# Second attention of a four-layer model: where batches 2 and 3 are summed and normalised, and in which order

## The reference

```python
x = x + _L0_ffn_ref(_layernorm(x, axis=-1), ...)            # the sum that ends layer 0
x = x + _L1_xattn_ref(ctx_1024, ctx_1024, _layernorm(x, axis=-1), mask, L1_xattn_Wv, ..., L1_xattn_bo)

def _layernorm(x, axis=-1, eps=1e-05):
    m = jnp.mean(x, axis=axis, keepdims=True)
    v = jnp.var(x, axis=axis, keepdims=True)
    return (x - m) / jnp.sqrt(v + eps)

def _L1_xattn_ref(values, keys, queries, mask, Wv, Wk, Wq, Wo, bo):   # 16 heads of 8 columns
    ...
    energy = jnp.where(mask == 0, jnp.float32(-1e+20), energy)
    attn = jax.nn.softmax(energy * (1.0 / E ** 0.5), axis=3)
    out = jnp.einsum('nhqk,nkhd->nqhd', attn, v).reshape(N, Sq, E)
    return out @ Wo.T + bo
```

## Time and profile before

| | us |
|---|---|
| median of three timed runs | 1225.13 |
| lowest and highest | 1221.35, 1225.40 |
| the profiled execution | 1229.93 |
| its span, first to last instruction | 1228.1 |
| TensorE busy in the span | 1054.8 (86%) |
| VectorE busy | 722.0 (59%) |
| ScalarE busy | 644.5 (52%) |
| GpSimd busy | 565.4 (46%) |
| mean granted clock of TensorE | 0.929 of full |

### The profile page before, as it was taken

How to read it: one execution, slowest core, us unless ns; L and a number is a source line. 1 busy time by engine, 2 the same in 40 slices (tenths; PEclk the granted TensorE clock), 3 DMA queues, 4 the chain that set the end, 5 groups by cost and what they waited for, 6 DMA issues and landing times.

```text
span 1228.1 us, 22204 instructions
## 1 busy us (share of the span) xinstructions
PE 1054.8 (86%) x6815; PEld 797.5 (65%) x6815; DVE 722.0 (59%) x2456; ACT 644.5 (52%) x2117; POOL 565.4 (46%) x918
## 2 busy tenths in 40 slices
PE   4988999669889978879999997776799999977994
PEld 3775789635556657756767665665667776654994
DVE  5574454487676772286767784322776676852444
ACT  2343333347778714358778762222387888731231
POOL 5223665350000152557555656365375555655452
PEclk9988999979999999899999997698799999986997
DMA  2003556589500124110000001363300000004666
GB/s 63 13 26 120 161 179 205 164 148 408 188 1 1 36 63 141 50 33 19 1 19 18 1 4 44 85 185 121 86 19 1 2 1 1 2 31 124 193 209 180
DMA packets 116004, 102.86 MB, mean 84 GB/s; under 512 B 18027, under 2 KB 97571, under 8 KB 115888
## 3 DMA queue, kind: packets, MB, share of 16 engines
q1 hardware_dynamic: 105280, 82.71, 23.1%
q0 software_dynamic: 8448, 17.20, 4.2%
q10 hardware_dynamic: 2160, 1.53, 0.5%
HBM read 65.04 MB, written 36.36 MB: 83 GB/s over the span
## 4 chain that ended last, share of the span: by engine, by line
PE 57%; DVE 17%; issue 6%; ACT 6%; another core or an unknown queue 4%; DMA 4%; POOL 3%; SPq 2%; DVEq 0%; ACTq 0%; POOLq 0%
PE ps L2952 4%; PE ps L2756 4%; PE ps L2758 4%; PE ps L2848 4%; PE ps L2757 4%; PE ps L2966 4%; PE ps L2861 4%; PE ps L3493 3%; PE ps L3497 3%; PE ps L3147 2%; PE ps L3506 2%; PE ps L2980 2%; ACT ex L1301 2%; DVE ln_st L1705 2%
## 5 line engine op out<-in xcount | busy, mean ns | idle before, releaser
L1301 ACT ACTIVATE ex<-ps,nmx 128x154 f32<-128x154 f32 x512 | 194.5, 393 | 73.9 <-DVE nmx L2257 72.3
L1085 POOL TENSOR_TENSOR pp<-ex,rc 128x256 f32<-128x256 f32 x256 | 157.7, 616 | 145.7 <-DVE rc L2262 144.8
L2257 DVE TENSOR_REDUCE nmx<-ps 128x2 f32<-128x308 f32 x256 | 119.5, 470 | 59.4 <-PE ps L2758 58.8
L922 POOL DMA_INDIRECT yq_d<-yq,ids_q x78 | 74.7, 958 | 79.5 <-DVE yq L2007 61.5
L2952 PEld LDWEIGHTS ps<-ident,pp 128*128 128x128 f32 x640 | 73.7, 141 | 56.5 <-POOL pp L1086 47.6
L2756 PE MATMUL ps<-kp,q_s 128*128 128x308 f32 x256 | 95.6, 374 | 12.9 <-ACT ex L1301 11.8
L1301 ACT ACTIVATION_READ_ACCUMULATOR ex<-ps,nmx 128x1 f32 x512 | 105.4, 206 | 0.0
L1418 ACT ACTIVATE pe<-ps,nmx 128x154 f32<-128x154 f32 x256 | 85.1, 394 | 37.1 <-DVE nmx L2138 36.0
L2952 PE MATMUL ps<-ident,pp 128*128 128x128 f32 x640 | 99.9, 280 | 3.8 <-POOL pp L1086 3.7
L892 POOL TENSOR_TENSOR ln_r<-ln_v,mhalf 128x4 f32<-128x4 f32 x32 | 33.2, 1036 | 112.3 <-DVE ln_v L1713 91.7
L2848 PE MATMUL ps<-xc_q,w_q 128*128 128x256 f32 (+1 forms) x276 | 63.5, 370 | 19.9 <-issue 13.8
(11 more groups left out here) (477 smaller groups left out, 2836.9 us busy)
## 6 DMA issues: line engine op xcount, KB each, us to landing
w_r<-in_L_ffn_W SPq DMA_DIRECT2D x69, 256.0 KB
xq_d<-blankq SPq DMA_DIRECT2D x4, 4160.0 KB, 23.8
w_q<-in_L_ffn_W SPq DMA_DIRECT2D x46, 256.0 KB
w_q<-in_L_ffn_w SPq DMA_DIRECT2D x46, 128.0 KB
xq<-xq_d SPq DMA_DIRECT2D x24, 130.0 KB
w_s<-in_L_ffn_W SPq DMA_DIRECT2D x8, 256.0 KB
w_e<-in_L_ffn_W SPq DMA_DIRECT2D x8, 256.0 KB, 4.7
acc<-yq_d SPq DMA_DIRECT2D x8, 256.0 KB, 4.4
```

The costliest lines, as they stand in the source:

```text
L922: pool.indirect_dma_start(yq_d[:, :], bass.IndirectOffsetOnAxis(ap=ids_q[:, c:c + 1], axis=0), yq[k % NY][:, h, :], None).then_inc(q_out[k ...
L1085: pool.tensor_tensor(pp[st % 2][:, m % 4, 2 * j:2 * j + 2, :], w[:, :, 0:P], r.broadcast_to([P, 2, P]), ALU.mult)
L1301: ins = act.activation(ex[:, tt % NEX, j, :], ps[:, tt % 3, j * SK:(j + 1) * SK], ACT.Exp, bias=nmx8[:, tt % 8, j:j + 1], accum_out=sm8[:, ...
L2257: dve.tensor_reduce(nmx8[:, tt % 8, :], ps[:, tt % 3, 0:2 * SK].rearrange("p (h s) -> p h s", h=2), AX.X, ALU.max, negate=True).then_inc(n ...
```

## The change

GpSimd adds batch 2's and batch 3's shares to `x_tok` (`whole_sum`) and writes their normalised rows (`normed`: power, product with `row_any`, subtraction of the mean, multiplication). VectorE keeps the statistics of these batches and waits for `x_new` in place of summing. VectorE packs batch 0's queries before it scales batch 1. The maxima and statistics are put in another order: batch 2's statistics behind the maxima of m = 2, batch 3's behind those of m = 6. Batch 1's transposes move behind the scores of m = 2, batch 2's to the end of step 0, and batch 3's into step 1, in front of `queries(2)`. The output bias is added in steps 1 to 4 (`out_bias`), and the blank rows are set in step 1.

```diff
--- before.py
+++ after.py
@@ -503,7 +503,7 @@
         ln_shift = z_bm
         c_hi_ok = sem("c_hi_ok"); c_ok = sem("c_ok")
         n_raw = [sem("n_raw0"), sem("n_raw1")]; n_wk0 = sem("n_wk0"); n_wo1 = sem("n_wo1"); n_wo = sem("n_wo"); n_zero = sem("n_zero"); n_kz = sem("n_kz")
-        n_x = sem("n_x"); n_xl = sem("n_xl")
+        n_n = sem("n_n"); n_xl = sem("n_xl")
         n_full = sem("n_full"); n_hi = sem("n_hi"); n_fa = sem("n_fa"); n_fd = sem("n_fd")
         n_s = sem("n_s"); n_m = sem("n_m"); n_e = sem("n_e"); n_r = sem("n_r"); n_z = sem("n_z")
         n_va = sem("n_va"); n_pv = sem("n_pv"); n_oh = sem("n_oh"); n_ol = sem("n_ol"); n_on = sem("n_on"); n_pr = sem("n_pr")
@@ -1086,20 +1086,42 @@
                     pool.tensor_tensor(pp[st % 2][:, m % 4, 4, :].rearrange("p (h c) -> p h c", h=4)[:, 2 * j:2 * j + 2, 0:SK - P],
                                        w[:, :, P:SK], r.broadcast_to([P, 2, SK - P]), ALU.mult).then_inc(n_z, 1)
 
+                def whole_sum(b):
+
+                    pool.wait_ge(p_add, B + 2 * (b - 1))
+                    pool.tensor_tensor(x_tok[:, tiles(b), :], x_tok[:, tiles(b), :], acc[:, bsl(b)].rearrange("p (n d) -> p n d", n=TB), ALU.add).then_inc(x_new, 1)
+
+                def normed(b):
+
+                    rstd(2, b)
+                    pool.wait_ge(ln_rstd, B * 2 + b + 1)
+                    pool.tensor_tensor(ln_r[:, tiles(b)], ln_r[:, tiles(b)], row_any[:, tiles(b)], ALU.mult).then_inc(n_n, 1)
+                    pool.tensor_tensor(xn_tok[:, tiles(b), :], x_tok[:, tiles(b), :], ln_mv[:, tiles(b), 0:1].broadcast_to([P, TB, D]), ALU.subtract).then_inc(n_n, 1)
+                    pool.wait_ge(n_n, 2 * (b - 1))
+                    pool.tensor_tensor(xn_tok[:, tiles(b), :], xn_tok[:, tiles(b), :], ln_r[:, tiles(b)].rearrange("p (n a) -> p n a", a=1).broadcast_to([P, TB, D]), ALU.mult).then_inc(ln_ok, 1)
+
+                def out_bias(b):
+
+                    pool.wait_ge(ln_ok, B * 2 + b + 1)
+                    pool.tensor_tensor(x_tok[:, tiles(b), :], x_tok[:, tiles(b), :], bo1[:, :].rearrange("p (a d) -> p a d", a=1).broadcast_to([P, TB, D]), ALU.add).then_inc(p_add, 1)
+
                 if l == 1:
                     rstd(2, 0)
                     pool.wait_ge(ln_ok, B * 2 + 1)
                     add_second(2)
                     rstd(2, 1)
+                    pool.wait_ge(ln_ok, B * 2 + 2)
+                    whole_sum(2)
                     add_second(3)
-                    rstd(2, 2)
-                    rstd(2, 3)
-                    for b in range(B):
-                        pool.wait_ge(ln_ok, B * 2 + b + 1)
-                        pool.tensor_tensor(x_tok[:, tiles(b), :], x_tok[:, tiles(b), :], bo1[:, :].rearrange("p (a d) -> p a d", a=1).broadcast_to([P, TB, D]), ALU.add).then_inc(p_add, 1)
-                    pool.memset(blankq[:, :, 0:D + 1], 0.0)
-                    pool.memset(blankq[:, :, D + 1:D + 2], float(2 * (SPARE + NRUN * RUN))).then_inc(q_blank, 1)
+                    normed(2)
+                    whole_sum(3)
+                    normed(3)
                     for st in range(NST):
+                        if 1 <= st <= B:
+                            out_bias(st - 1)
+                        if st == 1:
+                            pool.memset(blankq[:, :, 0:D + 1], 0.0)
+                            pool.memset(blankq[:, :, D + 1:D + 2], float(2 * (SPARE + NRUN * RUN))).then_inc(q_blank, 1)
                         if st >= 2:
                             pool.wait_ge(*full(l, ("pt", st - 2, 4)))
                         if st == NST - 1:
@@ -1459,17 +1481,16 @@
                 queries(0)
                 exps(0, 0)
                 exps(0, 1)
+                exps(0, 2)
                 xT_of(s, 1)
-                exps(0, 2)
                 exps(0, 3)
                 exps(0, 4)
                 queries(1)
                 exps(0, 5)
-                xT_of(s, 2)
                 exps(0, 6)
                 exps(0, 7)
                 copy_pt(0, 0)
-                xT_of(s, 3)
+                xT_of(s, 2)
                 for st in range(1, NST):
                     exps(st, 0)
                     out(st - 2)
@@ -1480,6 +1501,8 @@
                     copy_pt(st - 1, 2)
                     exps(st, 3)
                     exps(st, 4)
+                    if st == 1:
+                        xT_of(s, 3)
                     queries(st + 1)
                     exps(st, 5)
                     copy_pt(st - 1, 4)
@@ -2081,7 +2104,7 @@
                 def normal_first(b):
 
                     if b > 1:
-                        finish(1, b)
+                        dve.wait_ge(x_new, B + b + 1)
                     else:
                         first_share(b)
                         second_added(b)
@@ -2165,20 +2188,18 @@
                 scale(2, 0, x_tok, True)
                 second_added(1)
                 statistics(2, 1, x_tok)
-                normal_first(2)
+                queries(0)
                 scale(2, 1, x_tok, True)
-                queries(0)
                 maxima(0, 0)
                 maxima(0, 1)
-                scale(2, 2, x_tok, True)
-                normal_first(3)
                 maxima(0, 2)
+                normal_first(2)
                 maxima(0, 3)
                 maxima(0, 4)
                 queries(1)
                 maxima(0, 5)
-                scale(2, 3, x_tok, True)
                 maxima(0, 6)
+                normal_first(3)
                 maxima(0, 7)
                 for st in range(1, NST):
                     maxima(st, 0)
@@ -3217,17 +3238,16 @@
                 idle_products(0, 4)
                 scores(0, 0)
                 scores(0, 1)
+                scores(0, 2)
                 xT_of(s, 1)
-                scores(0, 2)
                 scores(0, 3)
                 scores(0, 4)
                 queries(1)
                 scores(0, 5)
-                xT_of(s, 2)
                 scores(0, 6)
                 transposes(0, 0)
-                xT_of(s, 3)
                 scores(0, 7)
+                xT_of(s, 2)
                 for st in range(1, NST):
                     scores(st, 0)
                     rest_values(st - 2)
```

## The result

The changed kernel takes 1219.36 us, the median of 13 runs (1214.48 to 1222.30), and the kernel before 1224.17 in 13 runs of the same job. The ratio is 0.9961, with a 95% interval of 0.9943 to 0.9979: between 2.6 and 7.0 us faster, 4.8 by the medians. The profiled execution took 1221.58 us, with a span of 1219.8 against 1228.1.

What follows compares the result with a forecast made beforehand. The second attention's entry was taken to be bound by VectorE, for which everybody waits. 4.4 us gained there less 1.3 given back in step 1 make 3.1, so the median 1225.13 becomes 1222.0 us, range 1221 to 1223.5.

Steps and rivals of the forecast that it cites:

- the entry: Start of the second attention, 245 to 285 us, where all wait for VectorE; shortening it should move all later steps equally.
- the outer one: The forecast's wider range, 1217.5 to 1228.5 us: down to fewer falls of the clock, up to four added ones.
- Scores and packing: At the attention's start: batch 0's queries packed from 255.7 instead of 259.25, first scores at 256.5 instead of 260.05.
- GpSimd's chain: GpSimd's new operations from batch 2's sum to batch 3's sum, starting at 257.8: 8.31 us, 8.8 with gaps.
- The chain comes last: In step 0 GpSimd, not VectorE, sets the end: batch 3's sum at 266.6, VectorE waiting about 1 us for it.
- the hinge: Start of step 0's last exponentials, after the maxima of m = 7: forecast at 268.6 against 273.00, 4.4 us earlier.
- The stall of the small variance operation: Batch 2's last statistics operation on VectorE, due at 260.5, held until GpSimd's addition ends at 261.6; costs nothing.
- Given back in step 1: Step 0's value products wait for ScalarE's copy of batch 3's transposes, behind the exponentials of m = 4: 1.3 us lost.
- At nothing: Four bias additions, 1.28 us at most each, cost nothing in steps 1 to 4, in GpSimd's idle 9.7 to 11.8 us.
- The sign that failed: The prediction would be wrong if the steps behind the entry aren't all moved by the same amount.
- The other rivals: Held-up chain 1226.2 us (0.06, larger loss 0.03); nothing given back in step 1, 1220.7 (0.12); no gain, 1225.1 (0.10).
- The clock's falls: Rival, TensorE's clock falls in other steps: two fewer, 1218.8 us (chance 0.12); two to four more, 1225.2 to 1228.5 (0.09).

Runs made afterwards that it cites:

- e3: Changed kernel with one more 128x512 broadcast multiplication on GpSimd between batch 2's rows and batch 3's sum; ratio to before 1.0002.
- e4: Changed kernel with ScalarE's copy of batch 3's transposes moved ahead of step 1's exponentials of m = 3; ratio to before 0.9970.
- e5: Changed kernel with the four bias additions and blank rows back in front of GpSimd's copy for step 0; ratio to before 0.9975.
- e8: Changed kernel with batch 3's copy early and GpSimd's product for batch 3 moved into its wait ahead of batch 2's sum; ratio to before 0.9943.
- e10: Changed kernel with six idle TensorE products inside the wait for packed keys in steps 2, 4, 5, 8, 9; ratio to before 0.9923.
- e1: Kernel before with only batch 0's query packing moved ahead of batch 2's sum and statistics and batch 1's scaling; ratio to before 0.9978.
- e7: Changed kernel with six idle TensorE products behind the wait for packed keys in steps 2, 4, 5, 8, 9; ratio to before 1.0007.
- e11: Kernel of e8 with six idle products for eight ahead of batch 0's transposes and two for three behind; ratio to before 0.9965.
- e9: Kernel before with six idle TensorE products inside the wait for packed keys in steps 2, 4, 5, 8, 9; ratio to before 0.9976.

## Why the prediction was right

- **Direction and size.** 3.1 us were forecast; 4.8 were measured (2.6 to 7.0), of which the trace puts 3.76 on the entry and step 1. Those 0.7 over the forecast are the entry's (below); the other 1.0 isn't attributed and lies well inside the interval. The measured 1219.36 is under my own range of 1221 to 1223.5, partly because the kernel before came out at 1224.17 and not 1225.13, and inside the outer one.
- **Scores and packing.** Forecast 256.5 and 255.7 on the clock of the kernel before; measured 256.34 and 255.54 (less 1.57). Part of this closeness is luck: in e3, e4, e5, e8 and e10 the packing came 0.25 to 0.72 later than here.
- **GpSimd's chain.** Forecast 8.8, measured 8.35. The mis-sized terms are the broadcast subtraction, 1.25 by the additions and 1.04 in fact, and the gaps between neighbours, 0.49 in the sum and about 0.2 in fact. The 128x4 product was 0.20, as the line through the earlier trace rows gave. For the subtraction the Trainium skill's estimate, 1.07 us (GPSIMD Engine Reference, Instruction dispatch), was nearer than my choice; for the additions of two full operands the trace says 1.26 again.
- **The chain comes last.** Forecast was a wait of VectorE of 1.1 for batch 3's sum; it was 1.07, and e3 showed that an operation added to the chain moves the hinge by its full length. The stall of the small variance operation, forecast at 1.1, was 1.02 (0.85 over its own time) and cost nothing. The exclusive lock of the Trainium skill's SBUF — State Buffer (Who interferes with whom) describes it, and e8 agrees: the same operation takes 0.17 where no GpSimd operation lies over it.
- **The hinge.** Forecast 4.4 earlier, measured 5.1: 0.45 by the shorter chain, 0.2 by its earlier start, 0.1 by the maxima. What was gained has more parts than my sum names: before, VectorE was held back by GpSimd for 2.2 us, of which my account names only 0.95, and up to 0.35 the half clock of the first scores before (the first pair of products takes 0.91 us there and 0.56 in e1, at the full clock).
- **Given back in step 1.** Forecast 1.3, measured 1.36; e4 took it away by moving one copy.
- **At nothing.** Steps 2 to 4 were unchanged by the additions, and e5 gives 0.26 for the other place.
- **The sign that failed.** It would be wrong, I wrote, if the steps behind weren't all moved by the same amount. Up to step 4 they were, by 3.76; behind step 5 it is 5.4 and behind step 9 7.0, by the two lengthened steps that only the kernel before had. Of the six waits that I counted for packed keys five are of 1.84; step 1's was 0.98 and is now 1.36.
- **The other rivals** fell by the same rows: no operation of the chain was held up, step 1 gave back 1.36, and the steps behind it moved with the entry.
- **Missing from the prediction.** The packing now hangs on TensorE's entry, which VectorE's work had covered before: the transposes of batch 0 wait 0.87 us behind idle products, and their clock moves the packing between 10.3 and 11.0 in the kernels with this entry (after, e3, e4, e5, e7, e8, e10), where it was 13.97 to 13.98 with the order before. e11 took 0.5 us of it back by the trace.
- **The clock's falls** were a rival. They fell differently in the two profiled executions, 3.3 us of the 8.3 between the spans. That the number of falls differs between the kernels was neither shown nor excluded.

## What to carry to other kernels

When work is moved off the engine that all wait for, follow the chain on the engine that takes it over: here that chain, not the early packing, set where the stage ended, and it could be shortened further by filling the wait in front of it. Ask next what the old cover had hidden: a copy behind two exponentials cost 1.36 us, idle products at the entry 0.5 by the trace, and each was mended by moving a line or dropping a few of the products. Compare such changes by distances inside the trace; the times of whole runs scatter by more than the parts are worth.

## What the runs showed of the hardware

- GpSimd's elementwise cost went by the operands and not by the operation: 1.04 us for 128x512 with one operand broadcast along the columns, subtraction and multiplication alike, and 1.25 to 1.28 for additions with two full operands or one broadcast over the tiles. A subtraction of two full operands stands elsewhere in the kernel before (line 1071, eight times) and took 1.30 at the median.
- A VectorE operation on four columns took up to 1.02 us when it met a GpSimd addition of 1.27, and 0.15 to 0.17 otherwise. VectorE's packing, which reads PSUM, took 0.75 either way.
- TensorE's granted clock fell from its full level to half after 1.84 us of waiting in some steps and not in others of the same kernel; there a fall made the step 1.6 us longer, while step 1 was as long at a granted clock of 0.87 as at 1.00 (9.04 us).
- The same kernel took 1171 us in one job and 1223 to 1231 in others. Its last part accounts for most of this: 751.6 us behind the attention in e9's profile, 805.1 in that of the kernel before.
